# A four-layer graph network on one core: three small matmuls of zeros ahead of each gathered visit, and the gathered rounds counted in registers

## The chip, the cores and the metric

The kernel runs on one core of a Trainium2 chip. The metric is the time on the device in microseconds (us), the median of several executions. The trace beside it is of one further execution, recorded by the hardware profiler. TensorE (PE) multiplies matrices, VectorE (DVE) does elementwise work and reductions, ScalarE (ACT) activations, GpSimd (POOL) issues the indirect transfers that gather rows, and SyncE (SP) issues plain transfers.
## The reference, cut to what matters

Four graph layers follow each other on 12,500 nodes with 64 features and 200,000 edges sorted by target; after each comes a residual and a layer norm. The change touches the second layer and the fourth, whose core is a sum over the edges of a node:

```python
messages = jnp.take(x, src, axis=0)                       # second layer
sum_msgs = jax.ops.segment_sum(messages, tgt, num_segments=num_nodes)
...
def sage_conv(x, src, dst, Wl, bl, Wr):                   # fourth layer, four times
    msg = x[src]
    agg = jax.ops.segment_sum(msg, dst, num_segments=N_NODES)
    deg = jax.ops.segment_sum(jnp.ones((src.shape[0], 1), x.dtype), dst, num_segments=N_NODES)
    agg = agg / jnp.maximum(deg, 1.0)
    return agg @ Wl.T + bl + x @ Wr.T
```

## The kernel before, in words

The program makes seven passes over the edges: gat, dev, gine, sage1, sage2, sage3 and sage4. Between gat and dev it builds a matrix that counts the edges from each node to each node of the first 49 tiles of 128 target nodes (KT = 49), and stores it in HBM as `counts`. Dev and the four sage passes use that matrix; they are called dense passes here, and only they are changed.

A dense pass goes over 49 target tiles, in 7 steps (STEPS) of 7 tiles (TB). The work on one tile is called a **unit**. For a unit, `dense_unit` (L921 to L936) multiplies 98 blocks of `counts` by the nodes' rows, in two halves of 49 blocks, each half in its own bank of PSUM (`ps_dense`). SyncE brings the blocks in pieces of 14 or 7 into `RING`, which holds one unit; a piece is loaded again once TensorE has used it (`piece_used`). Rows are cut into three bf16 parts, so a matmul has 3 x 64 = 192 columns in sage1 and sage4 and 3 x 32 = 96 in sage2 and sage3. Dev does its 49 tiles twice, with 49 blocks of 384 columns a unit each time, and gathers rounds in the first sweep alone. VectorE reduces each half and adds it (`take_dense`, L1769 to L1781).

Edges to other targets are gathered: 15 **rounds** a pass, each of 8 slots (SLOTS) of 512 edges. GpSimd gathers up to seven slots ahead. `cold_rounds` (L431) decides after each unit which rounds come now: it loads two neighbouring entries of the table `TURNS`, first and upto, and loops over the rounds between them. TensorE and VectorE each do this for themselves; VectorE between the two halves of its unit. At the end of a step all rounds that its nodes need are done. In a round, each slot goes through the target tiles that its edges reach; one slot and tile is a **visit**. In a visit VectorE makes a one-hot matrix (`hot`, L1729), waits for TensorE's sums of the visit before and adds them (`add`, L1736); TensorE waits for the one-hot matrix (`pair_hot`) and for the addition that frees its bank (`pair_acc`), and then does 12 matmuls (L962). All dense passes together have 845 visits in 75 rounds.

After each step of sage1 and sage3 `node_tensor` (L682) does that step's matrix products (L696, L703, L707). `settle` (L382) is an increment of a semaphore that nobody waits for, behind a wait.

Of the kernel before, what the change touches and what calls it, by code (L numbers as in the profile page):

```python
# [10 lines left out]
I32 = mybir.dt.int32  # L11
# [4 lines left out]
P = 128  # L16
# [16 lines left out]
TB = 7  # L33
# [14 lines left out]
WIDE_ROW = TILES * CHUNK  # L48
COLS = GROUPS * C
ROUND_COLS = SLOTS * C  # L50
AHEAD = 5
PIECES = [14, 14, 14, 7] * 2
PIECE_AT = [sum(PIECES[:j]) for j in range(len(PIECES))]
# [32 lines left out]
def build(nc, x, edge_attr, src_r, dst_r, dst_b, src_c, dst_c, w, out):  # L86
    ctx = ExitStack()
    with ctx:
# [158 lines left out]
        LASTS = sb("LASTS", [P, BLOCKS])  # L247
        TARGETS = sb("TARGETS", [P, STEPS + 1])
        INFO = sb("INFO", [P, 2], I32)
        TURNS = sb("TURNS", [P, KT + 1], I32)  # L250
        rangev = sb("rangev", [P, 2 * H])
        WIDE = sb("WIDE", [P, 1], I32)
        big = sb("big", [P, TB * H * D])
# [65 lines left out]
        ps_turn = psum("ps_turn", 2048)  # L319
        ps_hid = ps_turn[:, 0:1024]  # L320
        ps_dense = [ps_turn[:, 1024:1536], ps_turn[:, 1536:2048]]
        ps_out = psum("ps_out", 1024)
        ps_pair = psum("ps_pair", 1024)
        ps_agg = ps_pair[:, 0:512]
# [103 lines left out]
                eng.reg_load([reg for pair in spans[0:4] for reg in pair], SPAN[0:1, bass.ds(g, 4), :].rearrange("p a b -> p (a b)"))  # L428
            return span(eng, spans[s % 4])

        def cold_rounds(eng, u, r0, cold_round):  # L431

            first = eng.value_load(TURNS[0:1, bass.ds(u, 1)], min_val=0, max_val=ROUNDS)
            upto = eng.value_load(TURNS[0:1, bass.ds(u + 1, 1)], min_val=0, max_val=ROUNDS)
            with eng.If(first < upto):
                with eng.Fori(first, upto) as l:
                    cold_round(nc.s_assert_within(l + r0, 0, ROUNDS - 1, skip_runtime_bounds_check_because="upto <= ROUNDS - r0"))
# [285 lines left out]
        def _(pe):  # L723
# [24 lines left out]
            with pe.Fori(0, PAIRS) as b:  # L748
# [10 lines left out]
                        last = pe.matmul(ps_out[:, j * 2 * H:(j + 1) * 2 * H], bigT[0:D, j * P:(j + 1) * P], Wa[:, :], start=True, stop=True)  # L759
                last.then_inc(score_mm, 1)  # L760

            def pass_tensor(k):
                ps = passes[k]
                gat = ps["name"] == "gat"
# [152 lines left out]

            seen, turn, bank = pe.alloc_register("pe_pair"), pe.alloc_register("pe_turn"), pe.alloc_register("pe_bank")
            arrived = pe.alloc_register("pe_arrived")

            def dense_unit(k, t, u, srcs):  # L921

# [15 lines left out]
            def pass_dense(k):  # L938
# [5 lines left out]
                def cold_round(r):  # L944

                    pe.reg_add(arrived, arrived, 16 * C)
                    for s in range(SLOTS):
                        lo, hi = load_four(pe, spans, s, r * SLOTS + s)
                        pe.wait_ge(ps["gathered"][s], pe.snap(arrived, min_val=1, max_val=len(passes) * ROUNDS * 16 * C))
                        settle(pe)  # L950
                        with pe.Fori(lo, hi) as t:
                            pe.reg_add(seen, seen, 1)
                            count = pe.snap(seen, min_val=1, max_val=len(passes) * GROUPS * TILES)
                            pe.wait_ge(pair_hot, count)
                            settle(pe)
# [12 lines left out]
                r0 = pe.value_load(INFO[0:1, 0:1], min_val=0, max_val=ROUNDS - 1)  # L968
                if dev:
                    pe.wait_ge(chunk_read, CHUNKS + 2)  # L970
                    for q in range(2):
# [1 line left out]
                    last.then_inc(pair_agg, 1)  # L973
                    for half in range(2):
                        pe.wait_ge(xp_loaded, 16 * (xp_before[k] + half + 1))
                        with pe.Fori(0, KT) as u:
                            dense_unit(k, u, u + half * KT, SRC_HALF)
# [4 lines left out]
                with pe.Fori(0, STEPS) as b:  # L982
                    with pe.Fori(0, TB) as r:
                        u = b * TB + r
                        dense_unit(k, u, u, TILES)
                        cold_rounds(pe, u, r0, cold_round)
                    node_tensor(pe, k, b * 2)
                    node_tensor(pe, k, b * 2 + 1)

# [274 lines left out]
        def _(ve):  # L1264
# [319 lines left out]
            def build_vector():  # L1584
# [109 lines left out]
                shares = tmp[:, 0, 0:KT].rearrange("p (b r) -> p b r", b=STEPS)  # L1694
                shares_i = tmp[:, 1, 0:KT].bitcast(I32)
                for r in range(TB):
                    step(ve.tensor_scalar(shares[:, :, r], gain, float(r * 9363), None, ALU.mult))
                step(ve.tensor_copy(shares_i, tmp[:, 0, 0:KT]))
                step(ve.tensor_scalar(shares_i, shares_i, 16, None, ALU.arith_shift_right))
                step(ve.tensor_copy(tmp[:, 0, 0:KT], shares_i))  # L1700
                step(ve.tensor_tensor(shares, shares, TARGETS[:, 0:STEPS].unsqueeze(2).broadcast_to([P, STEPS, TB]), ALU.add))
                step(ve.tensor_copy(TURNS[:, 0:KT], tmp[:, 0, 0:KT]))
# [7 lines left out]

            pairs, turn, bank = ve.alloc_register("ve_pairs"), ve.alloc_register("ve_turn"), ve.alloc_register("ve_bank")
            prev, after = ve.alloc_register("ve_prev"), ve.alloc_register("ve_after")

            def pass_dense(k):

# [2 lines left out]
                per = node_steps[name]  # L1718
                step(ve.memset(acc, 0.0))
                r0 = ve.value_load(INFO[0:1, 0:1], min_val=0, max_val=ROUNDS - 1)  # L1720

                def take_indices(s, g):

# [59 lines left out]
                def unit(t, u, rounds):  # L1783

                    take_dense(t, u, 0)
                    if rounds:
                        cold_rounds(ve, t, r0, cold_round)
                    take_dense(t, u, 1)

                for s in range(SLOTS - 1):  # L1790
# [1 line left out]
                if name == "dev":  # L1792
                    with ve.Fori(0, STEPS) as b:
                        step.loop(b, per + 1)
                        with ve.Fori(0, TB) as r:
                            unit(b * TB + r, b * TB + r, True)
                        flush()
# [8 lines left out]
                    return  # L1806
                with ve.Fori(0, STEPS) as b:
                    step.loop(b, 2 * per + 1)
                    with ve.Fori(0, TB) as r:
                        unit(b * TB + r, b * TB + r, True)  # L1810
                    flush()
# [50 lines left out]
```

## Time and profile before

| what | value |
|---|---|
| median of 3 executions | 11548.31 us (11543.83 to 11570.66) |
| the profiled execution, its own time | 11566.34 us |
| its span in the trace | 11564.5 us |
| busy PE, PEld, DVE, ACT, POOL | 61%, 46%, 45%, 15%, 49% |
| mean granted TensorE clock | 0.74 of 2.4 GHz |

Times in the rows below are counted from the span's start. Gat, the building of the counts and gine fill 0 to about 4575 us and 5880 to 7930 us; dev lies between these, and the four sage passes fill the time from 7930 us to the end. In a row of the time line, the bracket tells how long the engine was idle ahead of the instruction and what ended the wait; "issue" is time in which it waited for nothing that the profile shows. In a row of a stretch the engines stand in the order PE, PEld, DVE, ACT, POOL, each with its busy time and its number of instructions; then come the granted TensorE clock as a share of 2.4 GHz, the mean busy share of the DMA engines and GB/s. The duration of matmuls in a row is from the first one's start to the last one's modelled end.

### The profile page before, as it was taken

The numbers are of one execution on the slowest core, as the hardware profiler recorded it, in microseconds if no ns is written. First come the engines' busy times: TensorE is split into PE (matmuls) and PEld (weight loads), VectorE is DVE, ScalarE is ACT, GpSimd is POOL, SyncE is SP. The second block draws the span as 40 slices with busy tenths as digits, with TensorE's granted clock in tenths as the row PEclk, the third lists the DMA queues.
The fourth block names the chain that finished last, engine by engine and source line by source line (L and its number), as shares of the span: only waits on it lengthen the run. The fifth ranks groups of instructions, "written<-read, shape, count | busy, mean of one in ns | idle before, by whom it ended". The sixth has DMA issues, their size and how long they took to land.

```text
span 11564.5 us, 251765 instructions
## 1 busy us (share of the span) xinstructions
PE 7105.4 (61%) x60627; PEld 5266.1 (46%) x60628; DVE 5149.2 (45%) x13946; ACT 1762.4 (15%) x3566; POOL 5676.9 (49%) x5555
## 2 busy tenths in 40 slices
PE   5676766664476666778854445455666555555666
PEld 4555555554122112455533344445555444444566
DVE  4555555555887776444322233333322333232333
ACT  2333333332133454000000000000000000000000
POOL 4777756553000001652047777776542765543754
PEclk6777777776888999888965555667777666666777
DMA  2333222221012234555532222224555666555566
GB/s 61 72 72 74 69 67 66 63 62 52 22 67 89 122 133 160 153 152 171 175 88 52 54 57 56 58 59 146 186 183 188 220 223 239 183 183 197 200 221 203
DMA packets 977745, 1416.35 MB, mean 122 GB/s; under 512 B 540705, under 2 KB 649761, under 8 KB 970914
## 3 DMA queue, kind: packets, MB, share of 16 engines
q1 hardware_dynamic: 689858, 1130.79, 28.8%
q0 software_dynamic: 184832, 224.29, 8.9%
q10 hardware_dynamic: 102752, 58.62, 1.7%
q14 instruction: 282, 2.31, 0.1%
q8 instruction: 21, 0.34, 0.0%
HBM read 1197.73 MB, written 215.36 MB: 122 GB/s over the span
## 4 chain that ended last, share of the span: by engine, by line
PE 31%; issue 22%; DVE 16%; DVEq 13%; POOL 12%; DMA 3%; ACT 1%; SPq 0%; POOLq 0%; ACTq 0%
PE ps_turn L934 14%; POOL ARENA L631 12%; PE ps_out L787 6%; PE ps_turn L891 4%; DMA ARENA<-counts 2%; PE ps_pair L787 2%; DVE onehots L1729 2%; DVEq L1743 2%; DVE ARENA L1644 2%; DVE ARENA L1646 2%; PE ps_pair L962 1%; PE ps_turn L703 1%; PE ps_out L707 1%; DVEq L395 1%; DVEq L1651 1%
## 5 line engine op out<-in xcount | busy, mean ns | idle before, releaser
L631 POOL DMA_INDIRECT ARENA<-table_sage,idx x1920 | 1895.3, 987 | 1737.6 <-DVE idx L1724 1198.8
L934 PE MATMUL ps_turn<-ARENA 128*128 128x96 bf16 (+2 forms) x24010 | 2275.5, 263 | 540.5 <-DVE DSUM L1775 216.9
L934 PEld LDWEIGHTS ps_turn<-ARENA 128*128 128x128 bf16 x24010 | 1869.0, 106 | 941.8 <-issue 638.7
L631 POOL DMA_INDIRECT ARENA<-table_gat,idx x1568 | 1743.3, 1112 | 885.4 <-issue 459.8
L631 POOL DMA_INDIRECT ARENA<-table_gine,idx x1568 | 1535.9, 980 | 965.1 <-issue 954.7
L891 PE MATMUL ps_turn<-ARENA 128*128 128x392 bf16 (+1 forms) x4204 | 1067.7, 360 | 667.8 <-DVE ARENA L1646 372.0
L631 POOL DMA_INDIRECT ARENA<-table_dev,idx x480 | 483.6, 1008 | 1753.6 <-DVE idx L1724 1617.3
L962 PE MATMUL ps_pair<-ARENA,onehots 128*128 128x32 bf16 (+2 forms) x10140 | 708.2, 229 | 993.7 <-DVE ARENA L1736 834.5
L787 PE MATMUL ps_out<-ARENA,onehots 128*128 128x256 f32 (+1 forms) x3136 | 937.9, 468 | 510.5 <-DMA ARENA<-table_gine,idx 368.5
L1644 DVE TENSOR_SCALAR ARENA<-ARENA 128x784 bf16<-128x784 f16 (+1 forms) x2102 | 1008.0, 480 | 360.3 <-issue 227.1
L962 PEld LDWEIGHTS ps_pair<-ARENA,onehots 128*128 x10140 | 581.3, 118 | 1126.3 <-issue 1125.2
L787 PE MATMUL ps_pair<-ARENA,onehots 128*128 128x256 f32 (+1 forms) x3136 | 846.0, 432 | 387.2 <-DMA ARENA<-table_gine,idx 290.5
L1775 DVE TENSOR_REDUCE DSUM<-ps_turn 128x128 f32<-128x384 f32 (+2 forms) x588 | 229.9, 391 | 1755.1 <-PE ps_turn L934 1645.6
L787 PEld LDWEIGHTS ps_out<-ARENA,onehots 128*128 128x128 f32 x3136 | 718.4, 285 | 620.7 <-issue 548.4
L891 PEld LDWEIGHTS ps_turn<-ARENA 128*128 128x128 bf16 (+1 forms) x4204 | 336.7, 101 | 1398.7 <-issue 1353.2
L1729 DVE SCALAR_TENSOR_TENSOR onehots<-DST,TBASE,COL 128x512 f32 x845 | 636.5, 753 | 642.5 <-issue 641.7
L787 PEld LDWEIGHTS ps_pair<-ARENA,onehots 128*128 128x128 f32 x3136 | 653.6, 261 | 485.8 <-issue 428.7
L1086 ACT ACTIVATE ARENA<-ps_turn 128x784 f32 x784 | 645.9, 824 | 1078.6 <-PE ps_turn L891 1078.3
L1043 ACT ACTIVATE bigT<-ps_turn 128x896 f32<-128x896 f32 (+1 forms) x42 | 38.4, 915 | 3451.8 <-PE ps_turn L696 3451.8
L1463 DVE TENSOR_TENSOR ARENA<-ARENA,ps_out 128x261 f32 (+1 forms) x584 | 205.7, 354 | 760.5 <-PE ps_out L787 757.2
L1646 DVE TENSOR_SCALAR ARENA<-ARENA 128x128 bf16<-128x128 f16 (+1 forms) x2102 | 520.7, 248 | 0.0
L1031 ACT ACTIVATE tmp<-COL,dst_in 128x128 bf16<-128x128 f32 x1568 | 495.4, 386 | 0.0
(300 smaller groups left out, 6458.9 us busy)
## 6 DMA issues: line engine op xcount, KB each, us to landing
ARENA<-counts SPq DMA_DIRECT2D x1470, 448.0 KB
counts<-ARENA SPq DMA_DIRECT2D x49, 3136.0 KB, 9.0
ARENA<-counts SPq DMA_DIRECT2D x490, 224.0 KB
ARENA<-dst_b SPq DMA_DIRECT2D x393, 256.0 KB
ARENA<-edge_attr SPq DMA_DIRECT2D x390, 128.0 KB, 2.5
ARENA<-table_sage,idx POOLq DMA_INDIRECT x1920
ARENA<-table_gat,idx POOLq DMA_INDIRECT x1568
ARENA<-table_gine,idx POOLq DMA_INDIRECT x1568
```

The lines of the kernel that those rows point to most:

```text
L631: pool.indirect_dma_start(ps["buf"][:, s, c, 0:ps["row"]], None, ps["table"][:, :], bass.IndirectOffsetOnAxis(idx[:, s, c:c + 1], 0)).then ...
L787: last = pe.matmul(sums[:, 0:H * D if gat else n], lhs, rhs, start=(c == 0 and q == 0), stop=(c == C - 1 and q == parts - 1))
L891: last = pe.matmul(ps_turn[:, at:at + WIDE_ROW // 2], marks[:, 0:P], marks[:, P + q * (WIDE_ROW // 2):P + (q + 1) * (WIDE_ROW // 2)], star ...
L934: last = pe.matmul(ps_dense[half][:, 0:n], RING[:, b, :], XP[:, b, :], start=(b == PIECE_AT[pieces[0]]), stop=(j == pieces[-1] and b == PI ...
L962: last = pe.matmul(sums, hot[:, c * P:(c + 1) * P], buf[:, s, c, q * n:(q + 1) * n], start=(c == 0 and q == 0), stop=(c == C - 1 and q == 2))
L1031: act.activation(distance[:, c * P:(c + 1) * P], COL[:, :], ACT.Abs, scale=-1.0, bias=dst_in[:, s % 2, c:c + 1]).then_inc(hot_distance, 1)
L1086: act.activation(to[:, :, c * CHUNK:(c + 1) * CHUNK].rearrange("p (q b) v -> p q b v", q=2), sums.rearrange("p q (b v) -> p q b v", v=CHUN ...
L1644: ve.tensor_scalar(marks[:, P:P + WIDE_ROW], IOTA16, BASES[:, bass.ds(q, 1)], KEY_pad[:, bass.ds(j, 1)], ALU.add, ALU.is_equal).then_inc(r ...
L1646: ve.tensor_scalar(marks[:, 0:P], COL16, AKEY_pad[:, bass.ds(j, 1)], None, ALU.is_equal).then_inc(ready, 1)
L1729: return ve.scalar_tensor_tensor(ring, DST[:, bass.ds(cols, C)].unsqueeze(2).broadcast_to([P, C, P]), TBASE[:, bass.ds(t, 1)], COL[:, :].u ...
L1743: with ve.Fori(lo, hi) as t:
L1775: ve.tensor_reduce(DSUM[:, half, 0:n], ps_dense[half][:, 0:3 * n].rearrange("p (q v) -> p v q", q=3), X_AXIS, ALU.add).then_inc(dense_read, 1)
```

## The change

It has two parts. First, `fill(3)`: three matmuls of a zero matrix by 256 columns of zeros stand ahead of TensorE's wait for `pair_hot` in each visit. They write into `ps_turn[:, 0:256]`, in a bank that the dense passes use only in `node_tensor`. Second, the table `TURNS` is gone. VectorE stores for each of the seven steps how many rounds it gains (`GAINS`, already multiplied by 9363); each engine loads one such number at a step's start and from then on works out first and upto by additions and a shift in registers. The rounds fall on the same units as before. TensorE's loop over dev's 49 units becomes a loop of 7 in a loop of 7, as VectorE's was.

```diff
+TURN_SHARE = (1 << 16) // TB + 1
-        TURNS = sb("TURNS", [P, KT + 1], I32)
+        GAINS = sb("GAINS", [P, STEPS], I32)
+        ps_fill = ps_turn[:, 0:2 * P]
-        def cold_rounds(eng, u, r0, cold_round):
-
-            first = eng.value_load(TURNS[0:1, bass.ds(u, 1)], min_val=0, max_val=ROUNDS)
-            upto = eng.value_load(TURNS[0:1, bass.ds(u + 1, 1)], min_val=0, max_val=ROUNDS)
+        def begin_turns(eng, turns):
+            eng.reg_mov(turns[4], 0)
+
+        def begin_step(eng, turns, b):
+
+            gain, share, base, _, upto = turns
+            eng.reg_load([gain], GAINS[0:1, bass.ds(b, 1)])
+            eng.reg_mov(share, 0)
+            eng.reg_mov(base, upto)
+
+        def cold_rounds(eng, turns, r0, cold_round):
+
+            gain, share, base, first, upto = turns
+            eng.reg_mov(first, upto)
+            eng.reg_add(share, share, gain)
+            eng.reg_alu(upto, share, 16, ALU.arith_shift_right)
+            eng.reg_add(upto, upto, base)
+            first, upto = eng.snap(first, min_val=0, max_val=ROUNDS), eng.snap(upto, min_val=0, max_val=ROUNDS)
             with eng.If(first < upto):
                 with eng.Fori(first, upto) as l:
...
+            def fill(n):
+
+                for _ in range(n):
+                    pe.matmul(ps_fill, ZERO[:, :], ZEROS[:, 0:2 * P], start=True, stop=True)
+
...
                             count = pe.snap(seen, min_val=1, max_val=len(passes) * GROUPS * TILES)
+                            fill(3)
                             pe.wait_ge(pair_hot, count)
...
                 with pe.Fori(0, STEPS) as b:
+                    begin_step(pe, turns, b)
                     with pe.Fori(0, TB) as r:
                         u = b * TB + r
                         dense_unit(k, u, u, TILES)
-                        cold_rounds(pe, u, r0, cold_round)
+                        cold_rounds(pe, turns, r0, cold_round)
...
-                for r in range(TB):
-                    step(ve.tensor_scalar(shares[:, :, r], gain, float(r * 9363), None, ALU.mult))
...
-                step(ve.tensor_copy(TURNS[:, KT:KT + 1], TARGETS[:, STEPS:STEPS + 1]))
+                step(ve.tensor_scalar(gain, gain, float(TURN_SHARE), None, ALU.mult))
+                step(ve.tensor_copy(GAINS[:, :], gain))
```

```order
L934 MATMUL ps_turn<-ARENA 128x192 x49
L433 ISA
L433 TENSOR_LOAD TURNS
L433 ISA x2
L434 ISA
L434 TENSOR_LOAD TURNS
L434 ISA x2
L435 COMPARE_AND_BRANCH
L436 UNCONDITIONAL_BRANCH
L436 ISA
L428 TENSOR_LOAD SPAN
```

and this after it:

```order
L959 MATMUL ps_turn<-ARENA 128x192 x49
L449 ISA
L451 REGISTER_ALU
L452 ISA
L454 COMPARE_AND_BRANCH
L455 UNCONDITIONAL_BRANCH
L455 ISA
L430 TENSOR_LOAD SPAN
```

Two loads from memory and six register instructions have become three register instructions. VectorE has the same rows in the same place, behind its addition of the unit's first half.

In a visit of sage1 TensorE had, from the loop's head to its first matmuls:

```order
L951 UNCONDITIONAL_BRANCH
L952 ISA
L958 ISA
L962 MATMUL ps_pair<-ARENA,onehots 128x64 x3
L962 ISA
```

and now has:

```order
L976 UNCONDITIONAL_BRANCH
L977 ISA
L784 MATMUL ps_turn<-ZEROS 128x256 x3
L984 ISA
L988 MATMUL ps_pair<-ARENA,onehots 128x64 x3
L988 ISA
```

The three matmuls stand between the register that counts the visits (L977, before L952) and the waits for the one-hot matrix, which come ahead of L984 (before L958).

## Rows read from the trace of the kernel before

**Rows 1.** Most of sage1: stretch and length; busy us of the engines; clock; DMA.

```profile
7930.00:8800.00 870.00, 573.67 (x6238) 511.15 (x6238) 256.79 (x664) 29.19 (x52) 446.33 (x458) 0.74 0.55 186
```

**Rows 2.** Groups of PE's instructions, 7930 to 11565 us: busy, mean ns, idle before.

```profile
L934 PE MATMUL ps_turn<-ARENA 128*128 128x192 bf16 x9604 | 878.9, 257 | 164.7 <-DVE DSUM L1775 96.7 <-issue 38.7 <-DMA ARENA<-nodes_sage 29.4
...
L962 PE MATMUL ps_pair<-ARENA,onehots 128*128 128x64 bf16 x4056 | 271.8, 236 | 381.4 <-DVE ARENA L1736 320.6 <-issue 60.8
L962 PE MATMUL ps_pair<-ARENA,onehots 128*128 128x32 bf16 x4056 | 219.2, 193 | 463.0 <-DVE ARENA L1736 385.8 <-DVE onehots L1729 38.4 <-issue 33.6
```

**Rows 3.** Time line of PE in sage4: a unit, then a round's first visit.

```profile
11516.99 8.25 PE L934 MATMUL ps_turn<-ARENA 128*128 128x192 bf16 x98 [1.15 <-DVE DSUM L1775]
11527.25 0.65 PE L962 MATMUL ps_pair<-ARENA,onehots 128*128 128x64 bf16 x12 [2.02 <-issue]
```

**Rows 4.** Sage1, time line of PE, and its sequencer's lines between two units.

```profile
8118.48 8.24 PE L934 MATMUL ps_turn<-ARENA 128*128 128x192 bf16 x98 [1.16 <-DVE DSUM L1775]
8127.89 2.31 PE L934 MATMUL ps_turn<-ARENA 128*128 128x192 bf16 x26 [1.16 <-DVE DSUM L1775]
...
L433 PEldq FUSED_REGOPS  x2: 42/105/168, 8125.1 to 8125.6; - x2
...
L435 PEldq COMPARE_BRANCH  x1: 214/214/214, 8126.7 to 8126.7; - x1
```

**Rows 5.** Loads by the sequencers: duration min/median/max ns, first and last start.

```profile
L433 PEldq TENSOR_LOAD <-TURNS x245: 297/307/712, 4593.2 to 11523.7; - x123
...
L428 PEldq TENSOR_LOAD <-SPAN x150: 588/599/620, 4611.1 to 11536.8; - x150
```

**Rows 6.** Time line of DVE in sage1 ahead of a round's first visit.

```profile
7972.14 0.28 DVE L1779 SCALAR_TENSOR_TENSOR ARENA<-DSUM,FLAG,ARENA 128x64 f32 x1 [0.24 <-DVE DSUM L1775]
7975.50 0.75 DVE L1729 SCALAR_TENSOR_TENSOR onehots<-DST,TBASE,COL 128x512 f32 x1 [3.08 <-issue]
```

**Rows 7.** Two neighbouring visits of sage1: time lines of DVE and PE.

```profile
7985.78 0.75 DVE L1729 SCALAR_TENSOR_TENSOR onehots<-DST,TBASE,COL 128x512 f32 x1 [1.14 <-issue]
...
7987.09 0.75 DVE L1729 SCALAR_TENSOR_TENSOR onehots<-DST,TBASE,COL 128x512 f32 x1 [0.42 <-issue]
...
7987.08 0.82 PE L962 MATMUL ps_pair<-ARENA,onehots 128*128 128x64 bf16 x12 [1.75 <-DVE ARENA L1736]
7988.61 0.82 PE L962 MATMUL ps_pair<-ARENA,onehots 128*128 128x64 bf16 x12 [0.71 <-DVE ARENA L1736]
```

**Rows 8.** PE's sequencer in these two visits: the counting of the visit.

```profile
L952 PEldq FUSED_REGOPS  x2: 73/73/73, 7988.0 to 7989.8; - x2
```

**Rows 9.** Sage2 between rounds: a stretch, its plain transfers, a wait of PE.

```profile
9216.00:9245.00 29.00, 18.28 (x294) 16.86 (x294) 4.40 (x17) 0.95 (x3) 14.31 (x16) 0.82 1.05 393
...
q1 hardware_dynamic: 3769, 10.41, 92.4%
...
9220.72 0.76 PE L934 MATMUL ps_turn<-ARENA 128*128 128x96 bf16 x14 [1.35 <-DMA ARENA<-counts]
```

**Rows 10.** Stretches of visits: one of sage1, one of dev (columns as in rows 1).

```profile
8022.50:8038.30 15.80, 7.37 (x108) 5.98 (x108) 9.06 (x23) 0.00 (x0) 12.14 (x13) 0.50 0.14 35
...
4655.50:4677.30 21.80, 11.73 (x132) 9.50 (x132) 12.78 (x31) 0.00 (x0) 16.82 (x17) 0.84 0.33 103
```

**Rows 11.** Time line of PE: two visits of dev; sage1 and sage4 behind rounds.

```profile
4657.74 1.46 PE L962 MATMUL ps_pair<-ARENA,onehots 128*128 128x128 bf16 x12 [0.35 <-issue]
4660.10 0.84 PE L962 MATMUL ps_pair<-ARENA,onehots 128*128 128x128 bf16 x12 [0.91 <-DVE ARENA L1736]
...
4677.48 16.09 PE L934 MATMUL ps_turn<-ARENA 128*128 128x384 bf16 x98 [1.09 <-DVE DSUM L1775]
...
7997.72 9.79 PE L934 MATMUL ps_turn<-ARENA 128*128 128x192 bf16 x98 [1.15 <-issue]
...
11453.09 10.91 PE L934 MATMUL ps_turn<-ARENA 128*128 128x192 bf16 x98 [1.57 <-issue]
11468.34 9.90 PE L934 MATMUL ps_turn<-ARENA 128*128 128x192 bf16 x98 [4.34 <-DVE DSUM L1775]
```

More of the change, by code:

```diff
@@ L429, in load_four, with turn_registers @@
             return span(eng, spans[s % 4])
-        def cold_rounds(eng, u, r0, cold_round):
-            first = eng.value_load(TURNS[0:1, bass.ds(u, 1)], min_val=0, max_val=ROUNDS)
-            upto = eng.value_load(TURNS[0:1, bass.ds(u + 1, 1)], min_val=0, max_val=ROUNDS)
+        def turn_registers(eng, name):
+            return [eng.alloc_register(f"{name}_{q}") for q in ("turn_gain", "turn_share", "turn_base", "turn_first", "turn_upto")]
+        def begin_turns(eng, turns):
[12 more added lines that the diff above has]
+            first, upto = eng.snap(first, min_val=0, max_val=ROUNDS), eng.snap(upto, min_val=0, max_val=ROUNDS)
             with eng.If(first < upto):
@@ L919, in _ @@
             arrived = pe.alloc_register("pe_arrived")
+            turns = turn_registers(pe, "pe")
             def dense_unit(k, t, u, srcs):
@@ L968, in pass_dense @@
                 r0 = pe.value_load(INFO[0:1, 0:1], min_val=0, max_val=ROUNDS - 1)
+                begin_turns(pe, turns)
                 if dev:
@@ L975, in pass_dense @@
                         pe.wait_ge(xp_loaded, 16 * (xp_before[k] + half + 1))
-                        with pe.Fori(0, KT) as u:
-                            dense_unit(k, u, u + half * KT, SRC_HALF)
+                        with pe.Fori(0, STEPS) as b:
                             if half == 0:
-                                cold_rounds(pe, u, r0, cold_round)
+                                begin_step(pe, turns, b)
+                            with pe.Fori(0, TB) as r:
+                                u = b * TB + r
+                                dense_unit(k, u, u + half * KT, SRC_HALF)
+                                if half == 0:
+                                    cold_rounds(pe, turns, r0, cold_round)
                     return
@@ L982, in pass_dense @@
                 with pe.Fori(0, STEPS) as b:
+                    begin_step(pe, turns, b)
                     with pe.Fori(0, TB) as r:
@@ L985, in pass_dense @@
                         dense_unit(k, u, u, TILES)
-                        cold_rounds(pe, u, r0, cold_round)
+                        cold_rounds(pe, turns, r0, cold_round)
                     node_tensor(pe, k, b * 2)
@@ L1693, in build_vector @@
                 step(ve.tensor_tensor(gain, TARGETS[:, 1:STEPS + 1], TARGETS[:, 0:STEPS], ALU.subtract))
-                shares = tmp[:, 0, 0:KT].rearrange("p (b r) -> p b r", b=STEPS)
-                shares_i = tmp[:, 1, 0:KT].bitcast(I32)
-                for r in range(TB):
-                    step(ve.tensor_scalar(shares[:, :, r], gain, float(r * 9363), None, ALU.mult))
[L1698 to L1702, printed above, removed]
-                step(ve.tensor_copy(TURNS[:, KT:KT + 1], TARGETS[:, STEPS:STEPS + 1]))
+                step(ve.tensor_scalar(gain, gain, float(TURN_SHARE), None, ALU.mult))
+                step(ve.tensor_copy(GAINS[:, :], gain))
                 ve.sem_inc(info_ready, 1)
@@ L1712, in _ @@
             prev, after = ve.alloc_register("ve_prev"), ve.alloc_register("ve_after")
+            turns = turn_registers(ve, "ve")
             def pass_dense(k):
@@ L1720, in pass_dense @@
                 r0 = ve.value_load(INFO[0:1, 0:1], min_val=0, max_val=ROUNDS - 1)
+                begin_turns(ve, turns)
                 def take_indices(s, g):
@@ L1786, in unit @@
                     if rounds:
-                        cold_rounds(ve, t, r0, cold_round)
+                        cold_rounds(ve, turns, r0, cold_round)
                     take_dense(t, u, 1)
@@ L1794, in pass_dense @@
                         step.loop(b, per + 1)
+                        begin_step(ve, turns, b)
                         with ve.Fori(0, TB) as r:
@@ L1808, in pass_dense @@
                     step.loop(b, 2 * per + 1)
+                    begin_step(ve, turns, b)
                     with ve.Fori(0, TB) as r:
```

## The prediction, on record before the run

> **What bounds the kernel now.** I first read the busy time of one stretch. In most of sage1, 870 us long, TensorE is busy for 574, VectorE for 257 and GpSimd for 446, and the DMA engines carry 186 GB/s [rows 1]. Nothing is full, so the time lies in the waits between the engines; the changed passes hold about 4,900 of 11,564 us. I then read TensorE's idle time by group [rows 2]: 165 us ahead of the 192-column matmuls of the units, and 844 us (381 and 463) ahead of the visits of the four sage passes, where the matmuls themselves take 491 us.
>
> A time line shows what these pieces look like. A unit of sage4 takes 8.25 us and the next matmul comes 1.15 us behind it; the first visit of a round comes 2.02 us behind its unit [rows 3]. Transfers don't make these gaps: inside the unit the 98 matmuls run as one piece, at 8.25 / 98 = 0.084 us each. The sequencer's lines show the cause. In sage1 the matmuls that begin at 8118.48 end at 8126.7. At 8125.1, 1.6 us before, the sequencer has already handed over the last of them and turns to the table; it has finished with both entries at 8126.7 and only then goes on to the next unit, whose first matmul starts at 8127.89 [rows 4]. So the 1.6 us for two entries are hidden behind queued matmuls, and what follows is laid bare. If the 1.6 us shrink, the whole chain moves forward.
>
> The visits are sequencer work too. A visit's matmuls take 0.82 us and the next visit starts 1.53 us after it (7987.08 to 7988.61) where the slot stays the same [rows 7]. The one-hot matrix of the second was ready at 7987.09 + 0.75 = 7987.84, but TensorE's sequencer reached the counting of this visit only at 7988.0 [rows 8]: TensorE was late, by its own instructions. In the other visit of these rows, which opens a new slot, the matrix was ready at 7986.53 and the matmuls came 0.55 us later, about as soon as the two waits allow: there TensorE stood waiting. Both kinds repeat all through the rounds; I take two thirds of the 676 sage visits as late by TensorE, the rest as waiting for VectorE; in dev VectorE is mostly the later one.
>
> **The change part by part.**
>
> *Loads replaced by registers.* There are 245 pairs of entries on each engine, 0.307 us a load [rows 5], 1.6 us for the pair with its register instructions [rows 4]. What replaces them is three register instructions; the FUSED_REGOPS in rows 4 take 0.04 to 0.17 us each, so 0.35 us in all with the spaces between. That saves 1.25 us a unit on TensorE. On VectorE it saves as much: from its addition at 7972.14 + 0.28 to the first one-hot matrix pass 3.08 us [rows 6], of which the two entries are about 1.45. Both sides of the first visit come forward alike. The second number loaded there, SPAN at 0.6 us, comes twice a round; its 150 loads show that there are 75 rounds [rows 5], and it stays.
>
> Ahead of a round: 75 x 1.25 = 94, less a little in dev, -92 us.
>
> Between two units without a round: sage1 and sage4 have 98 units and 30 rounds, so 68 such borders. In seven of them, one a step in sage4, TensorE waits 4.34 us for VectorE, which is in the norm of the step before [rows 11]; that stays. Two more are at the start of a pass. At 59 borders the gap of 1.15 us nearly vanishes: -66 us. The check against rows 2: 59 x 1.15 = 68 of the 165 us idle there, the rest being the starts of passes (29), the seven waits (30) and the returns from rounds.
>
> The reserve for this is DMA. A unit loads 98 x 128 x 128 x 2 bytes = 3.21 MB, so 9.4 us a unit is 341 GB/s and 8.3 us is 387. In a stretch of sage2 the transfers are the limit: 393 GB/s, of which q1, the counts, moved 10.41 MB in 29 us, 359 GB/s, and TensorE waits for them [rows 9]. At that rate a unit takes 8.95 us while gathers run. But `RING` is full after each round, and a run of two to four units is short by some 0.65 us a unit against a reserve of several us; I take the gap as gained in full, and 9.4 - 8.95 = 0.45 a border as the lower bound. In sage2 and sage3 these borders (68) wait for transfers anyway; I take -10 us for those that don't.
>
> The Trainium skill (HBM Reference, Specifications (TRN2)) gives an effective 358 GB/s per core, and says that a core that streams alone gets well above it. By the first figure a unit could not take under 8.97 us and the -66 would be about -25; this trace shows 393 GB/s, the second case.
>
> The Trainium skill (DMA: Bandwidth & Descriptors, Latency and other measured facts) puts the floor of a tensor_load at about 600 ns. By that a pair would cost 2.2 us and the 75 rounds would give some 139 us; the trace has 307 ns for one register and 599 for eight, so its rows stand.
>
> *New at a step's start.* One load of GAINS a step on each engine, 35 in all at some 0.5 us with its register work, part of it behind matmuls: +5 us (0 to 18). The build has six VectorE steps fewer in a chain: -2 us. Dev's nested loop costs nothing while 384-column matmuls are queued.
>
> *The fills.* No row has them, so their cost is bounded. In the visits of sage2 and sage3 12 pairs of weight load and matmul take 219.2 / 338 = 0.65 us, of which the last lasts 0.19 [rows 2]: 0.041 us a pair, register work included. Three pairs then cost the sequencer 0.12 us. In the array 128 columns differ by (1.46 - 0.84) / 11 = 0.056 us between dev's visits at 1.2 and at 2.4 GHz [rows 11], so 256 columns take 0.11 us at the high clock and 0.22 at the low one, and three of them 0.33 or 0.66. Behind the fills the sequencer still has its waits and registers, from 7988.0 to 7988.61 about 0.5 us beyond the counting [rows 7, 8]. As in rows 4 it does these while the array works. So 0.12 + 0.5 = 0.62 against 0.66: the array's time is hidden in full at the high clock and nearly at the low one. What remains is 0.12 us where TensorE is late, and nothing where it waits. The bounds are 0 and, if nothing overlapped, 0.66. I take the low value, because rows 4 show the sequencer 1.6 us ahead of the array: 676 x 2/3 x 0.12 = 54, +5 for dev, and +10 for VectorE, whose next addition waits for sums that end up to 0.16 us later. In all +69 us. Queued behind the fills is only the visit; who waits for it is VectorE's `add`.
>
> *The clock.* In a stretch of sage1's visits the granted clock is 0.50, that is 1.2 GHz; in dev, with twice the columns, 0.84 in one round [rows 10]. At the low clock the matmuls of a sage1 visit don't lengthen the visit, since the sequencer sets it; the gain lies in the unit behind: 9.79 and 10.91 us there against 8.25, and 16.09 in dev, the full clock, behind four visits at the high one [rows 11]. With the fills a sage1 visit streams 768 + 768 columns, just as many as a dev visit without. So I expect sage1 and sage4 to alternate as dev does. There are 30 such units, 7 of them in sage4 ahead of the 4.34 us wait, which takes the gain back. The other 23 lose about 2 us, and I give back half: -23. Sage2 and sage3 stay below this and wait for transfers: -2.
>
> **The sum.** -92 - 66 - 10 + 5 - 2 + 69 - 25 = -121 us. The profiled execution took 11,566 us, so it would take 11,445. It lies 18 us above the median of 11,548; I put the change against the median: 11,428 us.
>
> **The rivals.** (1) *DMA takes the unit gaps.* Sage1 and sage4 run into the 359 GB/s of counts; for it speaks that their stretches between rounds are already near it, against it the full ring after each round. The borders give 59 x 0.45 = 27 instead of 66 and the clock's 25 turns into waits: 11,428 + 39 + 20 = 11,487. Chance 0.15. (2) *The clock stays high through the rounds.* The units behind rounds get all of 2 us (23 x 2 = 46, plus 30 at the last units before rounds in sage2 and sage3, plus the later fills' tails): about 60 us more, 11,368. Chance 0.13. (3) *The fills stand in line with the visit*: the waits begin only when the zeros are through. Then a late visit costs 0.33 to 0.66 more, 845 x 0.4 = 340 instead of 69: about 11,700, slower than before. It decides from 0.22 us a visit on (190 us saved elsewhere / 845). For it speaks that the visits are the tightest loop; against it rows 4. Chance 0.10. (4) *The loads were hidden anyway*: another wait, for VectorE's reduction (which the rows name as releaser), ends at the same time. Then only the fills remain, 11,600. Against it: VectorE reduces the first half, the bank that the next unit needs first, 4 us earlier. Chance 0.05. My forecast has 0.57.
>
> **How the numbers follow.** The forecast itself spans 11,370 to 11,490: the fills' 0 to 0.2 us a visit and the clock's 0 to -60. With rivals 1 and 2 the range is 11,335 to 11,540, and leaves out rivals 3 and 4 and their neighbours, some 0.17. About 0.3%, 35 us, is what a measurement of this kernel tells from no change. Faster by more: the forecast and rivals 1 and 2 less their tails, 0.81. Within: what rivals 1 and 4 and a half-serial fill leave there, 0.08. Slower: rival 3 and most of 4, 0.11.
>
> **What would show it.** Right: between units of sage4 the gap falls from 1.15 to about 0.1 us, and ahead of a round from 2.02 to 0.9; visits of the same slot start 1.65 us apart instead of 1.53, those of a new slot as before; units behind rounds in sage1 take 9 us on the mean. Wrong: visits 1.9 us apart or more in the same slot (rival 3), units that hold waits for `counts` in sage1 (rival 1), a clock at 1.0 through all of a round (rival 2), a gap between units that stays above 1 us (rival 4).

## The result, and the profile after

The changed kernel takes 11,387.1 us (median of 4, 11,376.6 to 11,398.2) where the kernel before takes 11,557.8 (median of 4). The ratio is 0.985, with a 95% interval of 0.984 to 0.987: 170 us faster. The forecast was 121 us, with a range that holds the result. The profiled execution took 11,376.6 us, 190 less than the profiled one of before, so the two traces differ by somewhat more than the medians.

The groups of TensorE's instructions in the sage passes of the changed kernel, 7875 to 11375 us, answer to [rows 2] (busy us, mean ns, idle before):

```profile
L959 PE MATMUL ps_turn<-ARENA 128*128 128x192 bf16 x9604 | 862.7, 255 | 103.6 <-issue 69.5 <-DVE DSUM L1801 33.8 <-DMA ARENA<-counts 0.2
L959 PE MATMUL ps_turn<-ARENA 128*128 128x96 bf16 x9604 | 556.1, 222 | 287.2 <-DMA ARENA<-counts 186.2 <-issue 74.2 <-DVE DSUM L1801 24.4
L784 PE MATMUL ps_turn<-ZEROS 128*128 128x256 bf16 x2028 | 483.4, 367 | 450.5 <-issue 431.1 <-DMA ARENA<-table_sage,idx 14.5
L988 PE MATMUL ps_pair<-ARENA,onehots 128*128 128x64 bf16 x4056 | 252.8, 220 | 3.3 <-DVE ARENA L1762 1.2 <-issue 1.0
L988 PE MATMUL ps_pair<-ARENA,onehots 128*128 128x32 bf16 x4056 | 188.4, 191 | 0.3 <-issue 0.2
```

Idle time ahead of the 192-column units fell from 165 to 104 us, and the waits for VectorE's reduction among it from 97 to 34. Ahead of the visits 844 us of idle time have become 451 ahead of the fills and 4 ahead of the visits; the fills, busy for 483 us, stand in the time that went. In the 96-column units the waits for `counts` rose from 73 to 186 us: what the gaps gave there, the transfers took.

The same places of the time line as in [rows 3] and [rows 4], in sage4 of the changed kernel:

```profile
11289.82 46.75 PE L959 MATMUL ps_turn<-ARENA 128*128 128x192 bf16 x560
11336.92 0.50 PE L784 MATMUL ps_turn<-ZEROS 128*128 128x256 bf16 x3 [0.34 <-issue]
11337.38 0.70 PE L988 MATMUL ps_pair<-ARENA,onehots 128*128 128x64 bf16 x12
```

560 matmuls run as one piece over what were five gaps of 1.15 us, at 46.75 / 560 = 0.083 us each. A round's first visit comes 0.81 us behind the unit (11336.57 to 11337.38), where it was 2.02.

TensorE's visits in sage1 after, to be held against [rows 7]:

```profile
8073.46 0.82 PE L784 MATMUL ps_turn<-ZEROS 128*128 128x256 bf16 x3 [0.35 <-issue]
8074.07 0.85 PE L988 MATMUL ps_pair<-ARENA,onehots 128*128 128x64 bf16 x12
8076.12 0.82 PE L784 MATMUL ps_turn<-ZEROS 128*128 128x256 bf16 x3 [1.21 <-issue]
8076.74 0.85 PE L988 MATMUL ps_pair<-ARENA,onehots 128*128 128x64 bf16 x12
8077.69 0.82 PE L784 MATMUL ps_turn<-ZEROS 128*128 128x256 bf16 x3
8078.30 0.85 PE L988 MATMUL ps_pair<-ARENA,onehots 128*128 128x64 bf16 x12
...
8081.65 0.50 PE L784 MATMUL ps_turn<-ZEROS 128*128 128x256 bf16 x3 [0.54 <-issue]
```

In the same slot, visits start 1.56 us apart (8076.74 to 8078.30), against 1.53 before. The three fills take 0.82 us at 1.2 GHz and 0.50 at 2.4, and hardly anything of it is seen: three pairs of weight load and matmul cost this visit 0.03 us, not the 0.12 of the forecast. It isn't this visit alone. The four sage passes have 616 spacings between visits of one round, and in the mean over them a visit starts 0.03 us later behind the one before: 0.02 in the 196 that stay in a slot and 0.04 in the 420 that open a new one. From the counting of a visit to the last register work ahead of its matmuls the sequencer takes 0.43 us (median of the 676 sage visits) without the fills and 0.45 with them.

The clock by stretches of the changed kernel, visits and units together (most of sage1; dev's first sweep):

```profile
core 0: us, PE busy (x) PEld busy (x) DVE busy (x) ACT busy (x) POOL busy (x), PEclk, DMA share, GB/s
8000.00:8700.00 700.00, 553.26 (x5653) 465.47 (x5652) 214.16 (x562) 29.64 (x51) 372.98 (x376) 0.79 0.55 192
4590.00:5260.00 670.00, 538.77 (x4233) 336.17 (x4230) 293.49 (x670) 3.92 (x10) 432.61 (x438) 0.96 0.54 163
```

Dev's first sweep runs at 0.96 of 2.4 GHz, where the same stretch had 0.82; sage1 went from 0.73 in the same stretch to 0.79.

This table adds up TensorE's time line by pass, in the profiled executions. A unit or a round counts from its first matmul to its last one's end; "between" is what lies between two units, "ahead" between a unit and the round behind it, "back" between a round and the next unit. The whole of a pass includes the matrix products behind its steps, so the columns need not add up to it. With the change a round begins with its first fill, ahead of the visit's matmuls. That moves 7 us a sage pass and 18 us in dev, 47 in all, from "ahead" to "rounds".

| pass | whole | units | between | ahead | rounds | back |
|---|---|---|---|---|---|---|
| dev | 1284 to 1243 | 837 to 834 | 71 to 61 | 33 to -2 | 334 to 329 | 10 to 21 |
| sage1 | 1008 to 941 | 430 to 427 | 45 to -1 | 30 to 7 | 296 to 306 | 9 to 9 |
| sage2 | 757 to 744 | 328 to 355 | 69 to 40 | 47 to 22 | 293 to 303 | 21 to 25 |
| sage3 | 949 to 935 | 318 to 355 | 68 to 32 | 48 to 22 | 295 to 307 | 11 to 10 |
| sage4 | 856 to 813 | 448 to 440 | 62 to 37 | 30 to 6 | 296 to 306 | 19 to 23 |

In all -178 us. Another 15 us lie ahead of dev, where the change touches a few instructions alone; the two executions differ there for reasons that the change doesn't explain.

### The profile page after: what moved, and what is told of

It is laid out like the page before. It is cut to its first block, busy times and chain, and to the rows that moved or that the text cites. A ratio compares the mean times of both kernels' runs of the same rounds, so it can differ in the third digit from the quotient of the medians.

```text
span 11374.8 us, 254650 instructions
## 1 busy us (share of the span) xinstructions
PE 7403.8 (65%) x63162; PEld 5354.6 (47%) x63163; DVE 5140.2 (45%) x13935; ACT 1761.9 (15%) x3566; POOL 5687.9 (50%) x5555
## 4 chain that ended last, share of the span: by engine, by line
PE 35%; issue 20%; DVE 14%; POOL 13%; DVEq 10%; DMA 6%; ACT 1%; SPq 1%; POOLq 0%; ACTq 0%
PE ps_turn L959 14%; POOL ARENA L650 13%; PE ps_out L811 6%; DMA ARENA<-counts 4%; PE ps_turn L915 4%; PE ps_turn L784 2%; PE ps_pair L988 2%; PE ps_pair L811 2%; DVE ARENA L1676 2%; DVE ARENA L1678 2%; PE ps_turn L722 1%; DVEq L397 1%; DVE onehots L1755 1%; PE ps_out L726 1%; DVEq L1683 1%
## 5 line engine op out<-in xcount | busy, mean ns | idle before, releaser
L959 PE MATMUL ps_turn<-ARENA 128*128 128x96 bf16 (+2 forms) x24010 | 2241.1, 258 | 498.9 <-DMA ARENA<-counts 200.4
L959 PEld LDWEIGHTS ps_turn<-ARENA 128*128 128x128 bf16 x24010 | 1824.5, 104 | 909.5 <-issue 598.4
L784 PE MATMUL ps_turn<-ZEROS 128*128 128x256 bf16 x2535 | 570.1, 350 | 534.5 <-issue 505.6
L988 PEld LDWEIGHTS ps_pair<-ARENA,onehots 128*128 x10140 | 514.5, 108 | 208.1 <-issue 156.1
L988 PE MATMUL ps_pair<-ARENA,onehots 128*128 128x32 bf16 (+2 forms) x10140 | 588.2, 209 | 20.9 <-DVE ARENA L1762 13.5
L784 PEld LDWEIGHTS ps_turn<-ZEROS 128*128 128x128 bf16 x2535 | 212.9, 112 | 678.6 <-issue 643.7
```

The source lines that it names most:

```text
L784: pe.matmul(ps_fill, ZERO[:, :], ZEROS[:, 0:2 * P], start=True, stop=True)
L959: last = pe.matmul(ps_dense[half][:, 0:n], RING[:, b, :], XP[:, b, :], start=(b == PIECE_AT[pieces[0]]), stop=(j == pieces[-1] and b == PI ...
```

## The experiments

The experiments ran on chips on which all of this is slower: the kernel before took 14,820 to 15,024 us there, not 11,550. None ran on a chip of the first kind. Ratios are to the kernel before on the same chip.

What is different there shows in the trace of the first experiment, the registers without fills. TensorE's time line in sage4:

```profile
13533.90 0.82 PE L988 MATMUL ps_pair<-ARENA,onehots 128*128 128x64 bf16 x12 [2.30 <-DVE onehots L1755]
13539.12 0.82 PE L988 MATMUL ps_pair<-ARENA,onehots 128*128 128x64 bf16 x12 [4.40 <-issue]
13551.14 0.82 PE L988 MATMUL ps_pair<-ARENA,onehots 128*128 128x64 bf16 x12 [11.21 <-DVE ARENA L1762]
...
13561.79 0.24 PE L959 MATMUL ps_turn<-ARENA 128*128 128x192 bf16 x1 [1.11 <-issue]
13563.18 0.24 PE L959 MATMUL ps_turn<-ARENA 128*128 128x192 bf16 x1 [1.15 <-issue]
13564.59 0.32 PE L959 MATMUL ps_turn<-ARENA 128*128 128x192 bf16 x1 [1.17 <-issue]
```

and VectorE's at the same time:

```profile
13537.89 0.75 DVE L1755 SCALAR_TENSOR_TENSOR onehots<-DST,TBASE,COL 128x512 f32 x1 [0.39 <-issue]
13548.83 0.22 DVE L1762 TENSOR_TENSOR ARENA<-ARENA,ps_pair  x1 [10.19 <-remote]
```

VectorE stands still for 10 us in front of an addition whose sums TensorE had ready at 13,539.9 (`remote` is a releaser that the profile can't name), and TensorE does single matmuls of one unit 1.1 us apart, waiting for nothing that the profile shows. The operations themselves take what they took on the first chip: 0.75 us a one-hot matrix, 0.82 a visit. The likeliest reading is that instructions reach the sequencers more slowly; that is argued and not shown, and what slows them isn't seen in any trace. The experiments tell what the two halves do there, and the traces show which of the mechanisms are the same.

**The registers alone** (`regs_only`, `_b`, `_c` and `_d` are one kernel, run on four occasions).

```diff
-                            fill(3)
```

> The rounds are counted in registers as in the change, but no fills stand in the visits. Theory A (the shorter sequencer work gives nearly all of the 170 us): about 150 us faster than before, since the units' gaps of sage1 and sage4 and the gaps ahead of rounds close as they did in the change, and only the clock's share of the visits and of the units behind rounds is missing; in the trace the gap between two units of sage4 is 0.1 us or less and the clock in sage1's visits is 0.5. Rival B (the clock that the fills lift gives a large part): 80 to 110 us faster. Rival C (the fills cost as much as they give): 170 us faster or more, as much as the whole change.

Measured 0.9913 (0.9899 to 0.9926), 136 us faster (14,692 and 14,828).

> The registers without the fills, on the chip that this call gets. Theory A on a chip that takes 11,550 us before: 150 us faster than before, 20 us short of the change. Rival B (the clock that the fills lift gives a large part): 80 to 110 us faster. Rival C (the fills cost as much as they give): as fast as the change. On a chip that takes 14,800 us: 130 us faster again.

Measured 0.9892 (0.9874 to 0.9909), 173 us faster (14,842 and 15,016).

> The registers without the fills once more, to have them on a chip that takes 11,550 us for the kernel before. There theory A: 150 us faster than before, 20 us short of the change; rival B (clock): 80 to 110 us faster; rival C (fills cost as much as they give): 170 us faster. On a chip that takes some 15,000 us: 130 to 170 us faster again.

Measured 0.991 (0.9895 to 0.9925), 135 us faster (14,686 and 14,821).

> Registers on both engines, no fills, as the partner of the run before on the same chip: 130 to 170 us faster than before on a chip of 15,000 us, 150 us on one of 11,550 us (theory A), where rival B (clock) says 80 to 110 and rival C 170.

Measured 0.9902 (0.9882 to 0.9921), 153 us faster (14,842 and 14,996).

**The fills alone** (`fills_only`, `_b`): the kernel before with `fill(3)` in each visit.

```diff
+                            fill(3)
                             pe.wait_ge(pair_hot, count)
```

> The kernel before with the three fills of 256 columns in each visit, and with the table TURNS still loaded from memory. Theory A: within 25 us of before, since the fills cost the sequencer some 0.03 us a visit (25 us in all) and the warmer units behind rounds give about as much back; dev's visits run at the full clock and dev gets some 20 us shorter. Rival B (clock): 60 to 90 us faster. Rival D (the fills are dear, and the registers gave more than they seem to have): 30 to 60 us slower.

Measured 1.0084 (1.0071 to 1.0098), 116 us slower (14,944 and 14,828).

> The fills without the registers, on the chip that this call gets. Theory A on a chip that takes 11,550 us before: within 25 us of before. Rival B (clock): 60 to 90 us faster. Rival D (the fills are dear): 30 to 60 us slower. On a chip that takes 14,800 us: 115 us slower again.

Measured 1.0064 (1.005 to 1.0078), 106 us slower (15,122 and 15,016).

**The change itself** on such a chip.

> The change itself, unaltered, beside the two halves of it on one chip. If this chip takes about 11,550 us for the kernel before: 170 us faster, as measured first. If it is one that takes 14,800 us (where the sequencers stand still for 3 to 10 us at places with nothing to wait for): the sum of the halves measured there, -0.9% for the registers and +0.8% for the fills, so within 30 us of before; were it 170 us faster there too, the halves would not add.

Measured 0.9928 (0.9914 to 0.9941), 115 us faster (14,901 and 15,016), beside 173 for the registers alone and -106 for the fills alone on the same chip. The expectation, within 30 us of before, failed. The halves measured there would add to 67, 48 us less than the change gave; with 20 to 26 us of uncertainty in each of the three numbers that is little more than noise. What follows: on these chips all of the gain comes from the registers, and rival B (the clock gives a large part) is out there, since the fills alone are a loss. Beside the registers the fills cost 59 us by the medians.

This doesn't carry over to the first chip as it stands, because the clock doesn't rise here as it did there. In the rounds the change's clock is 0.69 in dev and 0.59 in sage1, against 0.59 and 0.54 for the registers alone; on the first chip the rounds went from 0.62 to 0.97 in dev and from 0.53 to 0.75 in sage1.

How the registers work is the same on both kinds of chip. Sage4 in the trace of the fills alone, with the table still loaded:

```profile
14447.73 8.25 PE L940 MATMUL ps_turn<-ARENA 128*128 128x192 bf16 x98 [1.16 <-DVE DSUM L1782]
14457.15 8.24 PE L940 MATMUL ps_turn<-ARENA 128*128 128x192 bf16 x98 [1.18 <-DVE DSUM L1782]
```

and in that of the registers alone, second occasion:

```profile
14750.69 50.77 PE L959 MATMUL ps_turn<-ARENA 128*128 128x192 bf16 x588 [3.84 <-DVE DSUM L1801]
```

Six units run as one piece of 588 matmuls, without a single fill.

**Registers on TensorE alone.** VectorE keeps TURNS and its two loads (`loaded_rounds` is `cold_rounds` of before); no fills.

```diff
-                        cold_rounds(ve, turns, r0, cold_round)
+                        loaded_rounds(ve, t, r0, cold_round)
```

> No fills; TensorE counts the rounds in registers, VectorE still loads both entries of TURNS. It takes the forecast's register term apart. Theory A (TensorE's sequencer set the gaps, between units by itself, and ahead of a round with VectorE 0.75 us behind it): the gap between two units closes in full, the gap ahead of a round's first visit by 0.75 of 1.25 us, and the kernel is 30 to 45 us slower than with registers on both engines, which were 130 to 170 us faster than before on chips of 15,000 us. Rival H (VectorE's loads alone set what matters): as slow as before. Rival I (VectorE's loads don't matter): as fast as with registers on both.

Measured 0.9917 (0.99 to 0.9935) beside 0.9902 (0.9882 to 0.9921) for both engines on the same chip: 138 and 153 us faster. The medians lie 16 us apart, with intervals that overlap, so between the 30 to 45 of theory A and the 0 of rival I nothing is decided by the times. Rival H (VectorE's loads alone matter) is out. The time lines say more. Gaps between units close in full, as one piece of 588 matmuls in sage4 shows:

```profile
14752.82 51.94 PE L968 MATMUL ps_turn<-ARENA 128*128 128x192 bf16 x588 [5.28 <-DVE DSUM L1819]
14806.07 0.66 PE L997 MATMUL ps_pair<-ARENA,onehots 128*128 128x64 bf16 x12 [1.31 <-DVE ARENA L1780]
```

The first visit comes 1.31 us behind its unit here. Summed as in the table, the time ahead of rounds is 33, 20, 29, 28 and 19 us in dev to sage4, against 15, 12, 29, 29 and 12 with registers on both engines and 33, 30, 47, 48 and 30 in the trace of before. So in dev VectorE alone sets this gap, in sage1 and sage4 it keeps 7 to 8 of 18 us, and in sage2 and sage3 TensorE alone sets it; why the passes differ in this isn't shown.

**What of the fills costs time.** Four kernels, all with the registers. First, fills of 8 columns:

```diff
-                    pe.matmul(ps_fill, ZERO[:, :], ZEROS[:, 0:2 * P], start=True, stop=True)
+                    pe.matmul(ps_fill[:, 0:8], ZERO[:, :], ZEROS[:, 0:8], start=True, stop=True)
```

> The change with fills of 8 columns in place of 256: the sequencer has the same instructions, the array hardly any work. Theory A: the clock falls back to what it was before the change (visits of sage1 at 0.55, of dev at 0.65), so that the time is that of the registers alone plus the handing over of the instructions, at 0.02 to 0.04 us for 845 visits: 130 us faster than before. Rival B: 60 to 90 us faster, because the clock's share is gone. If it is as fast as the change, the clock gives nothing.

Measured 0.9948 (0.9936 to 0.996), beside 0.9913 for the registers alone: the narrow fills cost 53 us (14,745 and 14,692), as much as the wide ones did on the other occasion (59). So the array's time and the clock together make no difference that these runs can tell there, and most of the price seems to be one of instructions. Second, twice as many:

```diff
-                            fill(3)
+                            fill(6)
```

> The change with six fills of 256 columns in a visit in place of three. Sage1's visits then stream as many columns as dev's do in the change, where the clock stayed at 2.4 GHz. Theory A: sage1 and sage4 keep 2.4 GHz through their rounds, their units behind rounds take 8.25 us, and the time is 180 to 200 us below before (10 to 30 below the change); sage2 and sage3 gain little. Rival E: at 1.2 GHz six fills take 1.3 us of the array, more than the sequencer's time in a visit, so visits of sage2 and sage3 get longer by 0.3 us and more, and the time is 30 to 100 us above that of the change.

Measured 0.9956 (0.9943 to 0.9968), 73 us above the registers alone (14,765 and 14,692). Both theories missed: theory A promised less time than with three fills, and rival E 30 to 100 us more than with three, where the price of six is 14 to 20 us above that of three. TensorE's time line in sage1 of this kernel:

```profile
9911.80 0.83 PE L784 MATMUL ps_turn<-ZEROS 128*128 128x256 bf16 x6 [0.61 <-issue]
9912.46 0.51 PE L988 MATMUL ps_pair<-ARENA,onehots 128*128 128x64 bf16 x12
...
9931.96 1.46 PE L784 MATMUL ps_turn<-ZEROS 128*128 128x256 bf16 x6 [0.27 <-issue]
9933.21 0.85 PE L988 MATMUL ps_pair<-ARENA,onehots 128*128 128x64 bf16 x12
9933.87 1.47 PE L784 MATMUL ps_turn<-ZEROS 128*128 128x256 bf16 x6
9935.13 0.85 PE L988 MATMUL ps_pair<-ARENA,onehots 128*128 128x64 bf16 x12
9936.57 0.86 PE L784 MATMUL ps_turn<-ZEROS 128*128 128x256 bf16 x4 [0.59 <-issue]
9937.87 0.27 PE L784 MATMUL ps_turn<-ZEROS 128*128 128x256 bf16 x1 [0.45 <-issue]
9938.58 0.27 PE L784 MATMUL ps_turn<-ZEROS 128*128 128x256 bf16 x1 [0.44 <-issue]
9943.45 0.82 PE L988 MATMUL ps_pair<-ARENA,onehots 128*128 128x64 bf16 x12 [4.60 <-DVE ARENA L1762]
```

The first visit runs at 2.4 GHz. In the two behind it the clock is at 1.2, six fills take 1.46 us, and the visits start 1.92 us apart (9933.21 to 9935.13): here the array's time does lengthen the visit. In the one at 9,936 the six fills come apart, with 0.45 us in front of the last two: TensorE waited for nothing that the profile shows, and it stood in the fills themselves. Third, one fill:

```diff
-                            fill(3)
+                            fill(1)
```

> The change with one fill of 256 columns a visit in place of three. Theory F (what fills cost is their instructions, which the sequencer has to get, not their time in the array: fills of 8 columns cost as much as those of 256): on a chip that takes 15,000 us, a third of the 53 us that three fills cost there, so 15 to 20 us slower than the registers alone. Rival G (the array's time): the same third, but then fills of 8 columns should have been free. On a chip that takes 11,550 us before: dev's and sage1's visits get less clock than with three fills, and the time is within 10 us of the registers alone.

Measured 0.9931 (0.9919 to 0.9943) beside 0.991: 30 us for one fill (14,716 and 14,686), where either theory had a third of 53. One, three and six fills cost 30, 53 to 59 and 73 us. Each of these is uncertain by some 20 us, so that they grow is shown, and the shape of the growth is not.

The time lines tell more of what a visit pays. The second column is the mean spacing of visits within a round in the sage passes, of those spacings that are under 3 us and so hold no long standstill; the last two are the granted clock in the rounds.

| kernel | spacing, us | clock, dev | clock, sage1 |
|---|---|---|---|
| first chip: before | 1.84 | 0.62 | 0.53 |
| first chip: the change | 1.86 | 0.97 | 0.75 |
| other chips: registers alone (four traces) | 1.85 to 1.87 | 0.59 to 0.60 | 0.54 |
| one fill | 1.87 | 0.61 | 0.55 |
| three fills of 8 columns | 1.88 | 0.60 | 0.54 |
| three fills of 256 (the change) | 1.95 | 0.69 | 0.59 |
| six fills of 256 | 2.13 | 0.75 | 0.69 |

Some 400 of the 616 spacings are of this kind on the other chips. There the narrow fills add next to nothing to them, some 0.02 us. Three wide ones add 0.09, about 35 us in all, and six add 0.27, about 110 us. So for the wide fills the array's time is a part of the price there, and rival G (the array's time) is not out. Where the narrow fills' 53 us lie isn't shown: the standstills, 205 to 217 a trace, differ from trace to trace by more than that.

Last, fills in dev alone:

```diff
-                            fill(3)
+                            fill(3 if dev else 0)
```

> The change with its fills in dev's 169 visits alone; the 676 visits of the sage passes have none. Theory A (the fills cost and give next to nothing in sage, and shorten dev's visits by the clock): on a chip of 11,550 us as fast as the change within 15 us. Rival B (the clock in sage1 and sage4 matters): 30 us or more slower than the change there. On a chip of 15,000 us, where three fills everywhere cost 54 us against the registers alone: theory F (a price for each instruction that is run) says a fifth of that, 11 us; theory J (the price is paid in dev, whose units had 20 to 25 us more stalls there) says 30 us or more.

Measured 0.9903 (0.9889 to 0.9916), 149 us faster (14,876 and 15,024), where the registers alone had 0.9892 to 0.9913. So dev's fills cost nothing that shows. Theory F's 11 us fit; the run speaks against theory J (paid in dev, 30 us or more), but it has an uncertainty of 20 us and no run of the registers alone on its own chip beside it.

## Why the prediction was right, point by point

*What bounds it.* The reading of [rows 3] and [rows 4] held: the gaps were TensorE's sequencer, laid bare behind the last queued matmuls. Between units of sage1 and sage4 they close in the change, and on the other chips they close in the kernel without fills.

*Ahead of a round*, -92 us. The table gives -133, of which 47 went to the fills in front: -86. The gap was forecast at 0.9 us; it is 0.81 in the row shown and 0.90 on the mean of sage4's rounds.

*Between units*, -66 in sage1 and sage4 and -10 in sage2 and sage3. Measured -46 and -25, -71 in all, and in sage2 and sage3 -65 between units with +64 in the units: -1. Rival 1 did not come in sage1 and sage4: their units stay whole at 0.083 us a matmul, with 0.2 us of waits for `counts` in all. In sage2 and sage3 the transfers took everything, 186 us of waits.

*The fills*, +69. This is the term that was mis-sized. "Three pairs then cost the sequencer 0.12 us" took the spacing of matmuls in a visit, 0.041 us a pair, for the sequencer's cost. That was not what the sequencer pays: three pairs delay it by 0.02 us and the visit by 0.03. The split into two thirds late visits and one third waiting ones was wrong too. Only 196 of the 616 visits behind another stay in their slot, and those of a new slot, which were to stay as they were, moved by 0.04 us against 0.02. In the table the rounds go from 1514 to 1551 us, of which 47 are the fills in front. Without these they are 8 us shorter: 3 to 5 us longer in each sage pass, 23 shorter in dev. So +69 was forecast and -8 came. That the array's time is hidden behind the waits was right on this chip; rival 3 (in line with the visit) is refuted by the 1.56 us.

*The clock*, -25. The units gave 3 us in dev, 3 in sage1 and 8 in sage4: -14. A unit straight behind a round in sage1 takes 9.84 us on the mean, where it took 10.45; the sign of being right had been 9. Dev's visits kept 2.4 GHz and its rounds became 23 us shorter, which I had not counted. That the clock is the reason is argued: no kernel ran on this chip with the fills narrow. That sage1 and sage4 would alternate between both levels "as dev does" is what the rows show.

*The rest.* The returns from rounds got 19 us longer, 12 of them in dev, which no term had. In dev the matmuls of a visit take 0.42 us less, so the last visit of a round ends sooner and the same chain on the sequencer follows; that is 6 of the 12, the rest is open. The forecast was 121 and the traces give 190. Of the difference, 77 come from the fills, 15 from the stretch ahead of dev and 9 from gaps between dev's units, none of which was forecast. The other way went 19 of returns, 11 of the clock in the units, 6 ahead of rounds and some 4 between units. Some 8 more were gained in pieces that the table doesn't split, among them the starts of steps. So the time fell into the range because the register terms, 158 of the 190 us, were right; the fills' term was not, and the smaller misses, the clock and the returns on one side and the stretch ahead of dev on the other, nearly cancelled by luck.

What stays open: how much the fills give or take on a chip of the first kind, since no kernel without them ran on one. The table allows an estimate, if all of these are the fills' doing: the clock's share in the units (-14) and dev's rounds (-23) against 14 us in the sage rounds and the returns (+19), so close to nothing. Why fills alone cost 106 to 116 us on the other chips and 53 to 59 beside the registers is also open. On those chips the registers alone are the best version measured, 0.989 to 0.991 against 0.993 for the change.

## What to carry to other kernels

When an engine is idle between two busy pieces, look at what its sequencer does from the moment at which it hands over the last instruction. Here 1.6 us of that work were hidden behind queued matmuls and what came past them was the gap, though the view named VectorE as releaser. Values that follow from a rule can be worked out in registers and need no table in memory.

A saving in front of an engine is worth what the next limit leaves: the same microsecond a unit came through in full where transfers had reserve (sage1), and went into waits for them where the DMA engines were full (sage2 and sage3).

Matmuls of zeros that hold the clock up were cheap in the array's idle time on one chip, 0.03 us a visit, and raised the clock there. On the others they cost 53 to 59 us and raised it far less, so measure them apart from the rest of a change, and on the chip that counts.

## What the runs showed of the hardware

A register load from memory takes 0.31 us for one register and 0.60 for eight [rows 5], 0.8 us with the register work and the check around it.

Three more pairs of weight load and matmul held the sequencer up by 0.02 us a visit (0.43 to 0.45), while the array worked on them for 0.50 to 0.82 us; in long units the sequencer was 1.6 us, some 19 matmuls, ahead of the array [rows 4].

One program took 11,550 us on one chip and 14,820 to 15,024 on others, at the same durations of its operations, with gaps of 1 to 10 us for which the profile names no cause. A kernel's ratio to another differs between them: 0.985 and 0.993 for this change.
